# The retention stage of a nine-stage language tower: turns unrolled, normalising moved to groups of batches

## The chip, the cores and the metric

The kernel runs on one core of a Trainium2 chip. The metric is device time in microseconds (us), the median of several runs. The engines named below are TensorE (PE; its weight loads are PEld), VectorE (DVE), ScalarE (ACT), GpSimd (POOL) and SyncE (SP), whose queue issues the transfers (DMA) of this stage. SBUF is the on-chip memory, PSUM the banks that matmuls write.

## The reference, cut to what matters

The tower embeds 16 batches of 128 tokens with 192 features and adds eight blocks to them. The change is in the first of these, a retention block of 12 heads of 16 features:

```python
h = h + _L0_attn_ref(_layernorm(h, axis=-1), Wq, bq, Wk, bk, Wv, bv)

def proj(W, b):
    y = jnp.einsum('mse,fe->msf', x, W) + b
    return y.reshape(m, s, H, d).transpose(0, 2, 1, 3)
q, k, v = proj(Wq, bq), proj(Wk, bk), proj(Wv, bv)
decay = 1.0 / (1.0 + jnp.abs(i[:, None] - i[None, :]))
retention = jnp.einsum('mhsd,mhtd->mhst', q, k) * decay
out = jnp.einsum('mhst,mhtd->mhsd', retention, v) + k
mean = jnp.mean(out, axis=(2, 3), keepdims=True)
var = jnp.var(out, axis=(2, 3), keepdims=True)
out = (out - mean) / jnp.sqrt(var + EPS)
return out.reshape(m, s, e)
```

There is no softmax, so heads need no row maxima. Mean and variance are those of one head over all 128 tokens and 16 features. The last line reshapes (head, token, feature) into (token, feature) without turning it back, so that the rows of the result mix tokens of one head: this is what the exchange of heads is for.

## The kernel before, in words

Each stage of the program allocates its own tiles and semaphores, writes one program for each engine, and ends in a barrier of all engines. A normalising stage ahead of this one leaves the layer-normed rows transposed in `m.xt` (96 x 2 x 2048: features over partitions in two halves, tokens of all batches along the row). `retention_stage` then takes one batch a turn, 16 turns.

GpSimd copies the 128 columns of the batch from `m.xt` to `xs` (L848). TensorE's turn for batch b is `scores(b)`, `projections(b + 1)`, `outputs(b)`:

- `projections`: q and k, each three column groups by two halves of the features (L859, 12 records each, since a float32 matmul shows as two), and k with v beside it, token by feature, in `kv_ps` (L862, 4 records of 384 columns);
- `scores`: 12 matmuls with 16 rows, one for a head, at the partition offsets 0, 32, 64 and 96 (L872, 24 records);
- `outputs`: 12 matmuls of 128x128 weights and 16 columns (L882, 24 records), then the column sums of the normalisation through a matmul with `mean_w`, which holds 1/(128*16): the means after VectorE has summed (L886) and the variances after it has squared and summed (L889). Both wait on TensorE's queue, and what is behind them waits too.

VectorE's turn (`sequence`) multiplies the scores by the decay (L927, four operations), adds the three biases for the next batch (`biased`, L919 twice and L921), waits for outputs, adds k (L937), sums (L939), subtracts the mean (L941), squares (L942), sums (L943), adds epsilon (L945), takes the reciprocal of ScalarE's root (L909, L947), refines it (`newton_steps`, L156 to L160) and scales (L949). Then SP stores the batch's heads to DRAM in (head, token, feature) order (L837). After the last turn SP waits for all 16 stores and reads all of it back in the mixed order (L840), and VectorE adds it to the residual `m.h` (L959).

q, k and `ret` have one buffer each, `kv` two; `o` is one tile that each batch's store must leave before the next batch is written:

```python
v.wait_ge(o_ready, b + 1)
v.wait_ge(stored, 16 * b)
```

and outputs of b wait until b - 1 is normalised, since the means and variances lie in the same bank as the outputs:

```python
pe.wait_ge(ret_ready, b + 1)
pe.wait_ge(normed, b)
```

Of the kernel before, what the change touches and what calls it, by code (L numbers as in the profile page):

```python
# [11 lines left out]
ALU = mybir.AluOpType  # L12
# [784 lines left out]

def retention_stage(nc, m, a, scratch):
    with Stage(nc, "ret") as s:
# [8 lines left out]
        xs = s.sb("xs", [DC, 2, P])  # L808
# [4 lines left out]
        o = s.sb("o", [P, H0, HD0])  # L813
        sq = s.sb("sq", [P, H0, HD0])
        rs = s.sb("rs", [P, H0])
        rsq = s.sb("rsq", [P, H0])
        var, std = s.sb("var", [P, H0]), s.sb("std", [P, H0])
# [4 lines left out]
        w_in, xs_ready, proj_ready = s.sem("w_in"), s.sem("xs_ready"), s.sem("proj_ready")  # L822
        qkv_ready, sc_ready, ret_ready = s.sem("qkv_ready"), s.sem("sc_ready"), s.sem("ret_ready")
        o_ready, rs_ready, mean_ready = s.sem("o_ready"), s.sem("rs_ready"), s.sem("mean_ready")
        rsq_ready, var_ready, eps_added = s.sem("rsq_ready"), s.sem("var_ready"), s.sem("eps_added")
        std_ready, normed, stored = s.sem("std_ready"), s.sem("normed"), s.sem("stored")
        back_in, dve = s.sem("back_in"), s.sem("dve")
        block = s.block()

        @block.sync  # L830
        def _(sp):
            for dst, src in ((wq, "L0_wq"), (wk, "L0_wk"), (wkv, "L0_wkv"), (bq, "L0_bq"), (bk, "L0_bk"),
                             (bkv, "L0_bkv"), (decay, "decay"), (mean_w, "mean_w")):
                sp.dma_start(dst[:], a[src]).then_inc(w_in, 16)
            with sp.Fori(0, NB) as b:
                sp.wait_ge(normed, b + 1)
                sp.dma_start(scratch[bass.ds(b, 1)].rearrange("b h s d -> s (b h) d"), o[:]).then_inc(stored, 16)  # L837

            sp.wait_ge(stored, 16 * NB)
            sp.dma_start(back[:], scratch.rearrange("b h s d -> b (h s d)")  # L840
                         .rearrange("b (s e) -> s b e", e=D)).then_inc(back_in, 16)

        @block.gpsimd
        def _(pool):
            with pool.Fori(0, NB) as b:

                pool.wait_ge(proj_ready, b)
                nc.gpsimd.tensor_copy(xs[:], m.xt[:, :, bass.ds(b * P, P)]).then_inc(xs_ready, 1)  # L848

        @block.tensor  # L850
        def _(pe):
            pe.wait_ge(w_in, 16 * 8)
            def projections(b):
                pe.wait_ge(xs_ready, b + 1)
                pe.wait_ge(qkv_ready, b)
                for w, ps in ((wq, q_ps), (wk, k_ps)):
                    for g in range(HG):
                        for c in range(2):
                            nc.tensor.matmul(ps[:, g * P:(g + 1) * P], w[:, c, g * P:(g + 1) * P], xs[:, c, :],  # L859
                                             start=(c == 0), stop=(c == 1))  # L860
                for c in range(2):
                    last = nc.tensor.matmul(kv_ps[:, 0:2 * D], xs[:, c, :], wkv[:, c, :],  # L862
                                            start=(c == 0), stop=(c == 1))
                last.then_inc(proj_ready, 1)

            def scores(b):
                pe.wait_ge(qkv_ready, b + 1)
# [8 lines left out]
            def outputs(b, par):  # L876
                pe.wait_ge(ret_ready, b + 1)
                pe.wait_ge(normed, b)
                for g in range(HG):
                    for j in range(HJ):  # L880
                        hd = slice((g * HJ + j) * HD0, (g * HJ + j + 1) * HD0)
                        last = nc.tensor.matmul(o_ps[:, hd], ret[:, j, g * P:(g + 1) * P],  # L882
                                                kv[par][:, D + hd.start:D + hd.stop], start=True, stop=True)
                last.then_inc(o_ready, 1)
                pe.wait_ge(rs_ready, b + 1)
                nc.tensor.matmul(o_ps[:, 256:256 + H0], mean_w[:], rs[:], start=True, stop=True)\  # L886
                    .then_inc(mean_ready, 1)
                pe.wait_ge(rsq_ready, b + 1)
                nc.tensor.matmul(o_ps[:, 288:288 + H0], mean_w[:], rsq[:], start=True, stop=True)\  # L889
                    .then_inc(var_ready, 1)  # L890
# [8 lines left out]
            scores(NB - 2)  # L899
            projections(NB - 1)  # L900
            outputs(NB - 2, 0)
            scores(NB - 1)
            outputs(NB - 1, 1)

        @block.scalar
        def _(act):
            with act.Fori(0, NB) as b:
                act.wait_ge(eps_added, b + 1)
                nc.scalar.activation(std[:], var[:], ACT.Sqrt).then_inc(std_ready, 1)  # L909

        @block.vector
        def _(v):
            c = Chain(v, dve)
            v.wait_ge(w_in, 16 * 8)
            def biased(b, par):

                v.wait_ge(proj_ready, b + 1)
                for dst, ps, bias in ((q, q_ps, bq), (k, k_ps, bk)):
                    nc.vector.tensor_tensor(dst[:], ps[:, 0:HG * P].rearrange("p (g t) -> p g t", g=HG),  # L919
                                            along(bias[:], 2, [P, HG, P]), ALU.add)  # L920
                nc.vector.tensor_tensor(kv[par][:], kv_ps[:, 0:2 * D], bkv[:], ALU.add).then_inc(qkv_ready, 1)  # L921

            def sequence(b, par, more=True):
                c.round(b, 9)
# [7 lines left out]
                if more:  # L932
                    biased(b + 1, 1 - par)
                v.wait_ge(o_ready, b + 1)
                v.wait_ge(stored, 16 * b)
                heads = [P, H0, HD0]
                c.step(nc.vector.tensor_tensor(o[:], o_ps[:, 0:D].rearrange("p (h d) -> p h d", d=HD0),  # L937
                                               kv[par][:, 0:D].rearrange("p (h d) -> p h d", d=HD0), ALU.add))
                nc.vector.tensor_reduce(rs[:], o[:], AX.X, ALU.add).then_inc(rs_ready, 1)  # L939
                v.wait_ge(mean_ready, b + 1)  # L940
                c.step(nc.vector.tensor_tensor(o[:], o[:], along(o_ps[:, 256:256 + H0], 2, heads), ALU.subtract))  # L941
                c.step(nc.vector.tensor_tensor(sq[:], o[:], o[:], ALU.mult))  # L942
                nc.vector.tensor_reduce(rsq[:], sq[:], AX.X, ALU.add).then_inc(rsq_ready, 1)  # L943
                v.wait_ge(var_ready, b + 1)
                nc.vector.tensor_scalar(var[:], o_ps[:, 288:288 + H0], LN_EPS, None, ALU.add).then_inc(eps_added, 1)  # L945
                v.wait_ge(std_ready, b + 1)
# [2239 lines left out]
```

## Time and profile before

| | |
|---|---|
| Time, median of 3 runs | 3940.85 us (3937.39 to 3941.53) |
| Profiled execution | 3947.3 us, span 3945.4 us |
| Mean granted clock of TensorE | 0.806 |
| Busy, share of the span | PE 66%, PEld 41%, DVE 65%, ACT 38%, POOL 23% |
| Retention stage | from 67 us (first load issued) to 316 us (residual added) |

### The profile page before, as it was taken

The numbers are of one execution on the slowest core, as the hardware profiler recorded it, in microseconds if no ns is written. First come the engines' busy times: TensorE is split into PE (matmuls) and PEld (weight loads), VectorE is DVE, ScalarE is ACT, GpSimd is POOL, SyncE is SP. The second block draws the span as 40 slices with busy tenths as digits, with TensorE's granted clock in tenths as the row PEclk, the third lists the DMA queues.
The fourth block names the chain that finished last, engine by engine and source line by source line (L and its number), as shares of the span: only waits on it lengthen the run. The fifth ranks groups of instructions, "written<-read, shape, count | busy, mean of one in ns | idle before, by whom it ended". The sixth has DMA issues, their size and how long they took to land. (4 is left out here: it accounts for less than half of the span.)

```text
span 3945.4 us, 40861 instructions
## 1 busy us (share of the span) xinstructions
PE 2591.1 (66%) x13081; PEld 1614.0 (41%) x13128; DVE 2548.7 (65%) x5667; ACT 1513.9 (38%) x2746; POOL 895.5 (23%) x510
## 2 busy tenths in 40 slices
PE   2881999378888986599631112688989556665356
PEld 2771666233434333389411111323222445554345
DVE  4445232559999997211489997587787587787431
ACT  0000222166656652111114442677777244444211
POOL 2000000166776773367200000000000011011121
PEclk8775999689999997799855555899999777787568
DMA  1001100021111110511100000100000000000041
GB/s 34 8 7 39 67 0 0 28 86 43 43 43 43 43 43 0 148 40 39 46 0 0 0 0 1 50 1 1 1 1 1 28 1 1 1 1 1 25 133 48
DMA packets 59727, 108.45 MB, mean 27 GB/s; under 512 B 32253, under 2 KB 48091, under 8 KB 54331
## 3 DMA queue, kind: packets, MB, share of 16 engines
q1 hardware_dynamic: 53788, 94.44, 7.5%
q0 software_dynamic: 5760, 11.82, 1.0%
q8 instruction: 88, 1.44, 0.1%
q14 instruction: 91, 0.75, 0.1%
HBM read 92.17 MB, written 18.03 MB: 28 GB/s over the span
## 5 line engine op out<-in xcount | busy, mean ns | idle before, releaser
L1885 POOL TENSOR_TENSOR mam_st<-mam_du,mam_b_rows 128x1536 f32<-128x1536 f32 x128 | 439.4, 3439 | 172.1 <-PE mam_ysum L1954 171.6
L2115 DVE TENSOR_TENSOR_SCAN mam_st<-mam_da,mam_st 128x512 f32<-128x512 f32 x384 | 441.1, 1204 | 35.9 <-ACT mam_da L2055 18.2
L1650 DVE TENSOR_TENSOR cod_hp<-cod_hp,cod_gate 128x512 f32<-128x512 f32 x512 | 324.0, 681 | 122.5 <-ACT cod_hp L1517 120.5
L1954 PE MATMUL mam_ysum<-mam_st,held_ident 128*128 128x512 f32 x768 | 387.1, 644 | 2.2 <-DVE mam_st L2121 2.2
L1517 ACT ACTIVATE cod_hp<-cod_up,cod_b 128x512 f32<-128x512 f32 x512 | 318.8, 692 | 130.9 <-PE cod_up L1388 130.3
L2055 ACT ACTIVATE mam_da<-mam_delta,mam_decay 128x508 f32<-128x508 f32 x384 | 254.2, 683 | 184.7 <-DVE mam_st L2115 150.0
L2121 DVE TENSOR_TENSOR mam_st<-mam_st,mam_c_ps 128x1536 f32<-128x1536 f32 x128 | 224.4, 1753 | 17.2 <-PE mam_c_ps L1949 13.7
L470 DVE SCALAR_TENSOR_TENSOR held_h<-x_dn,held_gate,held_h 128x192 f32 x256 | 89.2, 410 | 225.2 <-PE x_dn L436 225.1
L1954 PEld LDWEIGHTS mam_ysum<-mam_st,held_ident 128*128 128x128 f32 x768 | 159.3, 207 | 169.3 <-issue 162.2
L425 PE MATMUL x_up<-x_xg,x_w 96*128 96x512 f32 x384 | 177.5, 600 | 55.4 <-ACTq L450 55.4
L311 POOL COPY held_xt<-n_cols 96x1024 f32 x32 | 34.3, 1074 | 776.3 <-ACT n_cols L292 776.3
L1388 PE MATMUL cod_up<-cod_zr,cod_w1r 96*128 96x512 bf16 x512 | 198.2, 387 | 15.6 <-ACT cod_hp L1517 9.7
L1393 PE MATMUL cod_gate<-cod_wt,cod_sel_g 128*128 128x512 bf16 x465 | 181.7, 391 | 39.3 <-DVE cod_hp L1650 38.7
L2390 DVE MATCH_REPLACE8 att_neg<-att_top,att_neg 128x128 f32<-128x128 f32 x768 | 201.1, 276 | 0.3 <-issue 0.3
L267 PE MATMUL n_turned<-held_ident,n_rows 128*96 128x128 f32 x256 | 51.4, 385 | 212.2 <-DVE n_rows L245 212.1
L2383 DVE MAX8 att_top<-att_neg 128x8 f32<-128x128 f32 x768 | 154.9, 279 | 22.6 <-ACT att_neg L2321 15.4
L2278 PE MATMUL att_wide<-held_ident,att_probs 128*128 128x128 f32 x192 | 45.1, 425 | 178.3 <-ACT att_probs L2333 178.3
L2227 POOL TENSOR_TENSOR att_probs<-att_se,att_neg 128x1536 f32<-128x1536 f32 x16 | 55.0, 3440 | 387.8 <-DVE att_neg L2390 387.8
L436 PEld LDWEIGHTS x_dn<-x_w,x_ht 128*128 128x128 f32 x768 | 128.2, 190 | 28.7 <-issue 28.7
L1409 PE MATMUL cod_comb<-cod_hp,cod_w 128*16 128x512 f32 x1024 | 137.2, 608 | 3.0 <-DVE cod_hp L1650 3.0
L458 ACT ACTIVATE x_ht<-x_up 128x512 f32<-128x512 f32 x96 | 57.3, 597 | 211.7 <-PE x_up L425 211.7
L436 PE MATMUL x_dn<-x_w,x_ht 128*128 128x192 f32 x768 | 134.7, 326 | 0.0
(519 smaller groups left out, 5443.4 us busy)
## 6 DMA issues: line engine op xcount, KB each, us to landing
mam_b_rows<-b_scratch SPq DMA_DIRECT2D x32, 1024.0 KB, 7.5
sw_w<-in_L_w SPq DMA_DIRECT2D x2, 4608.0 KB, 33.2
gr_w<-in_L_w SPq DMA_DIRECT2D x1, 5376.0 KB, 43.0
x_w<-in_L_w SPq DMA_DIRECT2D x2, 2304.0 KB
gr_w<-in_L_w SPq DMA_DIRECT2D x1, 4608.0 KB
slot_scratch<-in_slot_fresh SPq DMA_DIRECT2D x1, 3860.0 KB
gr_rows<-slot_scratch SPq DMA_DIRECT2D x40, 96.5 KB, 1.9
gr_w<-home_scratch SPq DMA_DIRECT2D x16, 192.0 KB, 4.4
```

Of the source, the lines that this page charges most:

```text
L425: last = nc.tensor.matmul(up[f % NUP][:], w1_sb[:, c, f, :], xg[:, c, :], start=(c == 0), stop=(c == 1))
L436: last = nc.tensor.matmul(dn[e % 2][:, t, 0:D], ht[e % 2][:, f, t * P:(t + 1) * P], w2_sb[:, f0 + f, :], start=(f == 0), stop=(f == tiles[ ...
L1388: nc.tensor.matmul(up[u % BANKS][:], w1r[:, sub, f * P:(f + 1) * P], zr[g % 2][:, sub, :], start=True, stop=True).then_inc(up_ready, 1)
L1393: nc.tensor.matmul(gate[u % BANKS][:], sel_g[:, code, :], wt[g % 2][:, 2 * sub + half, :], start=True, stop=True).then_inc(gate_ready, 1)
L1517: nc.scalar.activation(hp[step % HOLD][:, j, :], up[u % BANKS][:], ACT.Gelu_apprx_tanh, bias=b1[:, sub * HT + f:sub * HT + f + 1]).then_in ...
L1650: nc.vector.tensor_tensor(at, at, gate[u % BANKS][:], ALU.mult).then_inc(gated, 1)
L1885: nc.gpsimd.tensor_tensor(st[it % N_ST][:], du[r % 2][:], along(b_rows[:, p % RING, n % PIECE, :], 1, [P, MC, MT]), ALU.mult)\
L1954: last = nc.tensor.matmul(ysum[:, c, :], m.ident[:], st[it % N_ST][:, c, :], start=False, stop=(it % DS == DS - 1))
L2055: nc.scalar.activation(live(da[:, c, :], r % 2), live(delta[r % 2][:, c, :], r % 2), ACT.Exp, scale=decay[:, c, n:n + 1]).then_inc(exp_rea ...
L2115: nc.vector.tensor_tensor_scan(fs, fa, fs, 0.0, ALU.mult, ALU.add).then_inc(scanned, 1)
L2121: nc.vector.tensor_tensor(x[:], x[:], along(c_ps[:], 1, [P, MC, MT]), ALU.mult).then_inc(weighted, 1)
L2390: last = nc.vector.match_replace(rev, top[:, n, :], rev, -BIG)
```

## The change

All of it is in `retention_stage`.

- The loops over batches are written out. Batches form five groups (4, 4, 4, 2, 2), and `o` holds all 16 batches.
- TensorE reads `m.xt` in place; `xs` and GpSimd's program are gone.
- The biases of q and k are added by ScalarE while it copies out of PSUM (three operations of 128x128 each, a bias for each partition); kv's stays on VectorE. q, k and kv have semaphores of their own.
- A batch's outputs are only gathered in its turn. The sums of a group follow its last gather. Means on TensorE and `centre` on VectorE come in the turn after the group's last, variances, `roots` and `scaled` two turns after it, the addition to the residual four turns after it.
- SP stores the batches of a group when the group is scaled, waits for the stores, and reads the group back.
- The weights' loads are in another order, and q's matmuls wait only for `wq` and `bq`, k's for `wk` and `bk`.

```diff
+RET_GROUPS = (4, 4, 4, 2, 2)
...
+            for i in range(len(ends)):
+                sp.wait_ge(normed, i + 1)
+                for b in range(NB)[batches(i)]:
+                    sp.dma_start(scratch[b:b + 1].rearrange("b h s d -> s (b h) d"), o[:, b]).then_inc(stored, 16)
+                sp.wait_ge(stored, 16 * (ends[i] + 1))
+                sp.dma_start(back[:, batches(i), :], scratch[batches(i)].rearrange("b h s d -> b (h s d)")
+                             .rearrange("b (s e) -> s b e", e=D)).then_inc(back_in, 16)
-        @block.gpsimd
-        def _(pool):
-            with pool.Fori(0, NB) as b:
-
-                pool.wait_ge(proj_ready, b)
-                nc.gpsimd.tensor_copy(xs[:], m.xt[:, :, bass.ds(b * P, P)]).then_inc(xs_ready, 1)
...
-            def outputs(b, par):
+            def outputs(b):
                 pe.wait_ge(ret_ready, b + 1)
-                pe.wait_ge(normed, b)
+                pe.wait_ge(kv_kept, b + 1)
+                pe.wait_ge(o_added, b)
+                pe.wait_ge(mean_kept, sum(e <= b - 1 for e in ends))
+                pe.wait_ge(eps_added, sum(e <= b - 2 for e in ends))
...
+            pe.wait_ge(wq_in, 32)
             projections(0)
-            with pe.Fori(0, NB // 2 - 1) as i:
-                for par in range(2):
-                    b = 2 * i + par
-                    scores(b)
+            for b in range(NB):
+                scores(b)
+                if b - 1 in ends:
+                    means(ends.index(b - 1))
+                if b - 2 in ends:
+                    variances(ends.index(b - 2))
+                if b + 1 < NB:
                     projections(b + 1)
-                    outputs(b, par)
...
+            def keep_qk(b):
+                for dst, ps, bias, made, kept in ((q, q_ps, bq, q_made, q_kept), (k, k_ps, bk, k_made, k_kept)):
+                    act.wait_ge(made, b + 1)
+                    act.wait_ge(sc_ready, b)
+                    for g in range(HG):
+                        last = nc.scalar.activation(dst[:, g, :], ps[:, g * P:(g + 1) * P], ACT.Identity,
+                                                    bias=bias[:, g:g + 1])
+                    last.then_inc(kept, 1)
...
+            v.wait_ge(w_in, 64)
+            biased(0)
+            for b in range(NB):
+                decayed(b)
+                if b - 1 in ends:
+                    centre(ends.index(b - 1))
+                if b - 2 in ends:
+                    scaled(ends.index(b - 2))
+                if b - 4 in ends:
+                    add_back(ends.index(b - 4))
+                if b + 1 < NB:
+                    biased(b + 1)
+                gather(b)
+                if b in ends:
+                    sums(ends.index(b))
+            last = len(ends) - 1
+            centre(last)
+            scaled(last)
+            for i in range(len(ends)):
+                if ends[i] + 4 >= NB:
+                    add_back(i)
```

## Rows read from the trace of the kernel before

**Rows 1.** Windows: stretch, length, busy time (records) of each engine, PEclk, DMA share, GB/s.

```profile
108.00:135.00 27.00, 22.74 (x159) 20.80 (x158) 13.57 (x40) 0.42 (x2) 0.80 (x2) 0.75 0.06 7
```

**Rows 2.** Groups by shape, 64.5 to 318 us; after the second bar idle time before.

```profile
L927 DVE TENSOR_TENSOR ret_ret<-ret_sc,ret_decay 128x384 f32<-128x384 f32 x64 | 31.2, 550 | 1.7 <-PE ret_sc L872 1.5
...
L889 PE MATMUL ret_o_ps<-ret_rsq,ret_mean_w 128*128 128x12 f32 x32 | 9.6, 378 | 19.6 <-DVE ret_rsq L943 19.6
L919 DVE TENSOR_TENSOR ret_q<-ret_q_ps,ret_bq 128x384 f32<-128x384 f32 x16 | 8.9, 558 | 77.1 <-PE ret_kv_ps L862 77.1
...
L886 PE MATMUL ret_o_ps<-ret_rs,ret_mean_w 128*128 128x12 f32 x32 | 6.7, 283 | 14.7 <-DVE ret_rs L939 14.7
```

**Rows 3.** Timeline of one turn, TensorE's matmuls: start us, duration us.

```profile
109.87 1.66 PE L872 MATMUL ret_sc<-ret_q,ret_k 16*128 16x128 f32 x24
...
111.46 2.93 PE L859 MATMUL ret_q_ps<-ret_xs,ret_wq 96*128 96x128 f32 x12
...
114.18 2.40 PE L859 MATMUL ret_k_ps<-ret_xs,ret_wk 96*128 96x128 f32 x12
...
116.42 1.46 PE L862 MATMUL ret_kv_ps<-ret_wkv,ret_xs 96*128 96x384 f32 x4
...
117.71 2.75 PE L882 MATMUL ret_o_ps<-ret_kv,ret_ret 128*128 128x16 f32 x24
...
123.54 1.67 PE L872 MATMUL ret_sc<-ret_q,ret_k 16*128 16x128 f32 x24
```

**Rows 4.** Windows, short ones in which TensorE's granted clock moves.

```profile
81.50:82.00 0.50, 0.39 (x12) 0.39 (x16) 0.06 (x1) 0.00 (x0) 0.00 (x0) 0.92 0.00 0
...
88.80:92.20 3.40, 3.40 (x27) 2.97 (x25) 1.49 (x3) 0.00 (x0) 0.40 (x1) 0.99 0.00 0
92.40:95.60 3.20, 1.04 (x5) 0.83 (x5) 1.77 (x5) 0.00 (x0) 0.00 (x0) 0.50 0.00 0
...
116.00:116.50 0.50, 0.50 (x6) 0.50 (x6) 0.00 (x0) 0.00 (x0) 0.00 (x0) 0.95 0.00 0
...
123.00:123.50 0.50, 0.49 (x2) 0.49 (x2) 0.00 (x0) 0.00 (x0) 0.00 (x0) 0.50 0.00 0
```

**Rows 5.** Other stages: groups, a window and a timeline row of like operations.

```profile
L253 DVE TENSOR_TENSOR n2b_rows<-n2b_rows,n2b_shift 128x768 f32<-128x768 f32 x4 | 3.8, 958 | 0.1
...
L641 PE MATMUL gr_up<-gr_xs,gr_shared 97*128 97x128 f32 x960 | 115.1, 276 | 4.1 <-issue 4.1
...
1700.00:1800.00 100.00, 97.95 (x753) 95.00 (x752) 13.78 (x40) 19.44 (x40) 73.88 (x60) 1.00 0.14 41
...
2046.34 3.20 ACT L2712 ACTIVATE qh_x<-qh_sc,qh_down 128x128 f32<-128x128 f32 x12 [2.69 <-DVE qh_down L2783]
```

**Rows 6.** The stage's first microseconds: a window, then timeline rows.

```profile
69.00:70.00 1.00, 0.00 (x0) 0.00 (x0) 0.00 (x0) 0.00 (x0) 0.00 (x0) 0.50 1.03 323
...
73.20 2.93 PE L859 MATMUL ret_q_ps<-ret_xs,ret_wq 96*128 96x128 f32 x12 [9.30 <-DMA ret_mean_w<-in_mean_w]
...
78.49 1.47 PE L862 MATMUL ret_kv_ps<-ret_wkv,ret_xs 96*128 96x384 f32 x4
...
81.61 1.44 PE L872 MATMUL ret_sc<-ret_q,ret_k 16*128 16x128 f32 x24 [1.66 <-DVE ret_kv L921]
```

**Rows 7.** Timeline of the last batch and the exchange of heads.

```profile
291.45 5.31 PE L882 MATMUL ret_o_ps<-ret_kv,ret_ret 128*128 128x16 f32 x24 [2.46 <-DVE ret_ret L927]
296.79 0.36 DVE L937 TENSOR_TENSOR ret_o<-ret_o_ps,ret_kv 128x192 f32<-128x192 f32 x1 [5.40 <-PE ret_o_ps L882]
...
301.80 0.36 DVE L949 TENSOR_TENSOR ret_o<-ret_o,ret_rs 128x192 f32<-128x192 f32 x1
304.87 0.39 SPq L840 DMA_DIRECT2D ret_back<-heads_scratch  x1
312.63 3.36 DVE L959 TENSOR_TENSOR held_h<-held_h,ret_back 128x3072 f32<-128x3072 f32 x1 [10.47 <-DMA ret_back<-heads_scratch]
```

**Rows 8.** DMA: issues with size and median us to landing; one issue's duration.

```profile
gr_w<-home_scratch SPq DMA_DIRECT2D x16, 192.0 KB, 4.4
...
67.41 0.41 SPq L834 DMA_DIRECT2D ret_wk<-in_L_wk  x1
```

More of the change, by code:

```diff
@@ L795 @@
 HG, HJ = 3, 4
+RET_GROUPS = (4, 4, 4, 2, 2)
 def retention_stage(nc, m, a, scratch):
+    ends = [sum(RET_GROUPS[:i + 1]) - 1 for i in range(len(RET_GROUPS))]
     with Stage(nc, "ret") as s:
@@ L828, in retention_stage, with batches @@
         block = s.block()
+        def batches(i):
+            return slice(ends[i] + 1 - RET_GROUPS[i], ends[i] + 1)
         @block.sync
         def _(sp):
[L832 to L837, printed above, removed]
@@ L901, in _, with means, variances @@
-            outputs(NB - 2, 0)
-            scores(NB - 1)
-            outputs(NB - 1, 1)
+            def means(i):
+                n = RET_GROUPS[i] * H0
+                pe.wait_ge(rs_ready, i + 1)
+                nc.tensor.matmul(o_ps[:, 256:256 + n], mean_w[:], rs[:].rearrange("p b h -> p (b h)")[:, 0:n],
+                                 start=True, stop=True).then_inc(mean_ready, 1)
+            def variances(i):
+                n = RET_GROUPS[i] * H0
+                pe.wait_ge(rsq_ready, i + 1)
+                pe.wait_ge(o_added, min(ends[i] + 2, NB))
+                nc.tensor.matmul(o_ps[:, 320:320 + n], mean_w[:], rsq[:].rearrange("p b h -> p (b h)")[:, 0:n],
+                                 start=True, stop=True).then_inc(var_ready, 1)
@@ L905, in _ @@
+            pe.wait_ge(wq_in, 32)
+            projections(0)
+            for b in range(NB):
[5 more added lines that the diff above has]
+                if b + 1 < NB:
+                    projections(b + 1)
+                outputs(b)
+            means(len(ends) - 1)
+            variances(len(ends) - 1)
         @block.scalar
         def _(act):
-            with act.Fori(0, NB) as b:
-                act.wait_ge(eps_added, b + 1)
-                nc.scalar.activation(std[:], var[:], ACT.Sqrt).then_inc(std_ready, 1)
+            def keep_qk(b):
[6 more added lines that the diff above has]
+                    last.then_inc(kept, 1)
@@ L913, in _, with biased, decayed @@
             c = Chain(v, dve)
[L914 to L924, printed above, removed]
+            def biased(b):
+                v.wait_ge(kv_made, b + 1)
+                v.wait_ge(o_added, max(b - 1, 0))
+                nc.vector.tensor_tensor(kv[b % 2][:], kv_ps[:, 0:2 * D], bkv[:], ALU.add).then_inc(kv_kept, 1)
+            def decayed(b):
                 v.wait_ge(sc_ready, b + 1)
@@ L931, in sequence, with gather @@
                 last.then_inc(ret_ready, 1)
-                if more:
-                    biased(b + 1, 1 - par)
+            def gather(b):
                 v.wait_ge(o_ready, b + 1)
[L935 to L939, printed above, removed]
@@ L947, in sequence @@
-                c.step(nc.vector.reciprocal(rs[:], std[:]))
-                newton_steps(nc, c, rs[:], var[:], std[:])
-                nc.vector.tensor_tensor(o[:], o[:], along(rs[:], 2, heads), ALU.mult).then_inc(normed, 1)
-                c.end_round()
-            biased(0, 0)
-            with v.Fori(0, NB // 2 - 1) as i:
-                for par in range(2):
-                    sequence(2 * i + par, par)
-            sequence(NB - 2, 0)
-            sequence(NB - 1, 1, more=False)
-            v.wait_ge(back_in, 16)
@@ L959, in _, with sums @@
-            nc.vector.tensor_tensor(m.h[:], m.h[:], back[:], ALU.add)
+                nc.vector.tensor_tensor(o[:, b], o_ps[:, 0:D].rearrange("p (h d) -> p h d", d=HD0),
+                                        kv[b % 2][:, 0:D].rearrange("p (h d) -> p h d", d=HD0), ALU.add)\
+                    .then_inc(o_added, 1)
+            def sums(i):
+                n = RET_GROUPS[i]
+                v.wait_ge(o_added, ends[i] + 1)
+                nc.vector.tensor_reduce(rs[:, 0:n], o[:, batches(i)], AX.X, ALU.add).then_inc(rs_ready, 1)
@@ new lines, in centre @@
+            def centre(i):
+                n = RET_GROUPS[i]
+                heads = [P, n, H0, HD0]
+                x, part = o[:, batches(i)], sq[:, 0:n]
+                mean = o_ps[:, 256:256 + n * H0].rearrange("p (b h) -> p b h", h=H0)
+                v.wait_ge(mean_ready, i + 1)
+                nc.vector.tensor_copy(mid[:, 0:n], mean).then_inc(mean_kept, 1)
+                v.wait_ge(mean_kept, i + 1)
+                c.step(nc.vector.tensor_tensor(x, x, along(mid[:, 0:n], 3, heads), ALU.subtract))
+                c.step(nc.vector.tensor_tensor(part, x, x, ALU.mult))
+                nc.vector.tensor_reduce(rsq[:, 0:n], part, AX.X, ALU.add).then_inc(rsq_ready, 1)
```

95 lines of the change are left out of this document (55 added, 40 removed).

## The prediction

> **What bounds the kernel now.** I read the page first, and only to find the place: the retention stage runs from about 67 to 316 us of a span of 3945.4 us, so the change can touch 6% of the program, and everything below is read inside that stretch. Next I read the stretch by windows [rows 1]: in 27.00 us, two turns of the batch loop, TensorE is busy 22.74 us and VectorE 13.57 us, so TensorE sets the pace, at a mean granted clock of 0.75. Then the groups by shape [rows 2] show what its idle time is. The two small matmuls of the normalisation, means (L886) and variances (L889), are busy 6.7 + 9.6 us and TensorE sat idle 14.7 + 19.6 us ahead of them for VectorE: 50.6 us in 16 turns, 3.16 us of each. VectorE in its turn sat 77.1 us ahead of L919 for the projections; it is no bound. Then one turn in order of time [rows 3]: scores 109.87, q projection 111.46, k 114.18, kv 116.42, outputs 117.71 to 120.46, the two small matmuls, and the next scores at 123.54: a turn of 13.67 us. Last the half-microsecond windows [rows 4], for the clock: TensorE runs scores, q and k at 0.50 of full speed (1.2 GHz), the grant goes to 1.00 (2.4 GHz) at 116, deep in the dense projections, and it is back at 0.50 before the next scores.
>
> **The change, part by part.** The chain that sets the end goes from the weights' landing through TensorE's 16 turns to the exchange of heads. Three stretches are to be summed: front, turns, tail.
>
> *Front.* Before, q waits until all eight loads have landed, at 73.20, while the queues move 323 GB/s [rows 6]. Now wq and bq come first and have a semaphore of their own. 288 KB at some 300 GB/s are 1 us behind the first traffic at 68, with bq behind it 69.5 to 70.5; k waits for wk and kv for the rest, each due while the part before it runs. So TensorE starts at about 70.2 instead of 73.2. Also the first scores started at 81.61, 1.65 us after kv had ended at 79.96, for VectorE's three bias additions; q and k now go to ScalarE as each is made, behind which the kv matmuls still run, and scores do not wait for kv's bias. 3.0 + 1.65 would be 4.6; I take 4.1, between 1.6 (the loads share the engines so that nothing lands early) and 4.7.
>
> *A turn of TensorE at either level of clock.* At the low level, from [rows 3, 7]: scores 1.6, q and k 2.7 + 2.5 (k's 2.24 ended at the high level), outputs 5.3 (the last batch, 291.45), kv twice its 1.29 at the high level, 2.6; together 14.7 us. At the high level: outputs 2.75 and kv 1.29 [rows 3], scores 0.78 (12 of 24 records in 0.39 [rows 4]), and q with k 24 records of 0.120 each, which is what 960 records of almost the same shape cost in another stage at a granted 1.00, 115.1 us [rows 5], so 2.88. Together 7.7 us. None of it changes in number: the same matmuls, read from the held transposed rows in place of the copy. The copy lay under scores and TensorE never waited for it; without it nothing is gained.
>
> *What leaves the turn.* Outputs of batch b no longer wait for b-1 to be normalised, and the small matmuls come once for a group, behind scores of the next turn. What is left of the 3.16 us: four times, means wait for the sums (after outputs, gather 0.36 [rows 7] and a sum over 768 elements, about 0.96 by the row of that size [rows 5], while scores run 0.8 to 1.6), then their two records and those of the variances, 0.4 to 0.6 each [rows 2]: 1.6 us for each of the four groups that end before the last turn, 6.4 us in all (1.2 to 1.9 each).
>
> *What VectorE now does.* Per batch: decay, four of 0.49 [rows 2], 1.95; kv bias 0.55, as L919; gather 0.36 [rows 7]. Per group of four: five operations over 768 elements and a share of the addition to the residual, six at 0.96 [rows 5], and some nine small ones of 0.17 to 0.25 with 0.04 between, 2.0, so 7.8, or 1.95 a batch. Sum 4.8, with the gaps 5.1 us a turn: below 7.7. The fullest turn (centring) has 1.95 + 0.17 + 2.9 + 0.55 + 0.36 = 5.9 and also fits. Behind centring stand the bias of kv and the gather; outputs of b+1 wait for both, a projection's length later. Outputs of b wait for the decay of b, 2.0 us behind scores, and the projections between last 4.2 or more. So the removed stall is not made again, except in turn 15, which has no projections: there scores, then a wait of 2.4 for decay and for the epsilon of the group before, then outputs, much as now [rows 7].
>
> *ScalarE* gets six 128x128 additions of a bias a turn. Twelve like it took 3.20 us elsewhere, 0.27 each [rows 5]: 1.6 us a turn on an engine that has only one root a turn now. The root of a group is queued ahead of the q and k of that turn and waits for VectorE until some 2.5 us behind scores; the last k is then kept 4.3 us behind scores, at the high level 3.4 us before the next scores ask. Cost nothing; if that cover were gone, 1 us in each of four turns.
>
> *SP's queue* carries the same 16 stores plus five reads back in place of one; each group's wait for its stores holds only SP, where the next store comes two turns later. Nothing but the last group's is on the path. The loops' removal is worth at most the 0.2 us of weight loads' issue a turn, which lies under matmuls; taken at nothing. That unrolled code feeds TensorE is seen in a stage written out flat: busy 97.95 of 100 us at 1.00 [rows 5].
>
> *The clock* is the unknown. If TensorE goes on at the mean of before, 0.75 [rows 1], a turn is 7.7/0.75 = 10.3 us, which agrees with 13.65 - 3.16 = 10.5. Its idle time is gone, though, and the dense projections return sooner, which speaks for more; against all of it speaks that between 88.8 and 92.2 TensorE was busy for the whole 3.40 us, the end of kv and then outputs with 16 columns each, and the next window reads 0.50 [rows 4]. Outputs and scores together are 3.5 us of such work in every turn. I take the middle of 7.7 and 10.3, 9.0 us, that is, one drop in most turns but a short one. The Trainium skill (TensorE: Matmul & The Clock Gate, Part 1) says that the low clock is the idle state and that sustained activity releases it. By that rule alone a TensorE that never idles is at the high level throughout; the row of 88.8 to 92.2 disagrees, and it is a rival below.
>
> *Turns, summed.* 15 x 9.0 = 135.0; four groups 6.4; last turn 1.6 + 2.4 + 4.0 = 8.0: 149.4 us from first scores to last outputs. Before: 81.61 to 296.76, 215.1 [rows 6, 7]. Gain 65.7.
>
> *Tail.* Before, 296.76 to 315.99 [rows 7], 19.2: 5.4 of normalising, store 2.7 with its handing over, read of all 16 batches 7.8, addition 3.36. Now two batches are normalised: five operations of 384 elements in place of 192 at +0.2 (0.56 for 384 in L919, 0.36 for 192 in L937 [rows 2, 7]) and one copy of 0.2, 6.6; two stores, 0.45 for the second's issue [rows 8] + 2.7, 3.1; a read of 192 KB, 3.2 (between the store's 2.7 for 96 KB [rows 7] and 4.4 for another read of 192 KB [rows 8]); addition 0.56. 13.5, gain 5.7 (4.4 to 6.5). Twelve batches' exchange and addition lie under turns.
>
> *Sum.* 65.7 + 4.1 + 5.7 = 75.5. The profiled execution took 3947.3 us (span 3945.4), so 3871.8 by its measure; the median of the runs is 3940.85, 6.4 lower, which the profiled one exceeds in stages the change leaves alone, so 3865.3: I say **3865 us**.
>
> **The rivals.** (1) *High clock throughout.* 15 x 7.7 = 115.5, groups 5.2, last turn 0.8 + 2.4 + 2.75 = 5.95: 126.7, gain 88.4 + 9.8 = 98.2, **3843 us**. For it: no idle time on TensorE, the flat stage at 1.00. Against: the drop after 88.8 to 92.2. (2) *The clock stays at three quarters.* 15 x 10.3 + 14.4 = 168.9, gain 46.2 + 9.8 = 56.0, **3885 us**. For it: the level falls in outputs and comes back only late in dense projections [rows 4], and both are in each turn still. (3) *A new wait on VectorE.* If centring, scaling and the kv bias queued ahead of the decay made outputs wait as in the last turn, 2.4 us a turn: 15 x 12.7 + 14.4 = 204.9, gain 10.2 + 9.8 = 20, **3921 us**. VectorE's 5.1 of 7.7 us speak against it. (4) *Slower.* The clock stays low: the one idle stretch that now never comes does not matter, but outputs and scores, nearer to each other, keep the grant at 0.50 in every turn. 15 x 14.7 + 6.8 + 9.3 = 236.6, 21.5 more, less 9.8: **3953 us**. It decides from a turn of 14.0 us on, so only when hardly any of the time is at the high level. Against it: at 116, as in each turn, dense projections did lift it [rows 4]. (5) *The change doesn't unhook the turns* (turn still 13.65, since some other wait ties outputs to the normalising): gain 9.8, **3931 us**.
>
> **How the numbers follow.** Forecast 0.42, (1) 0.21, (2) 0.25, (3) 0.05, (4) 0.03, (5) 0.03; 0.01 for the rest. The range from 3840 to 3888 takes the first three with the bounds of front (1.6 to 4.7), groups and tail; that is 0.88 less their own edges. A measurement of this kernel tells about 0.2%, 8 us, from no change: all of the first three and (3) and (5) are faster by more; between (5) and (4) lies what is within it. Faster 0.94, same 0.02, slower 0.04.
>
> **What would show it.** No idle time of TensorE ahead of the small matmuls but in four turns (some 3 us in all, 34.3 before); turns of 7.7 to 10.5 us, falling together with the granted clock of their window; VectorE's idle time, now ahead of the gather, for outputs; the first q at about 70; the last read landing 3 us after its issue, 6 us after the last scaling. I am wrong if the granted clock of the stage stays at 0.75 or goes to 1.00, if ScalarE loads a table between roots and additions, or if outputs wait for decay outside of the last turn.

## The result and the profile after

The changed kernel takes 3873.2 us (median of 4 runs, 3866.7 to 3882.2), the kernel before 3941.2 (4 runs); the ratio is 0.9828 with a 95% interval of 0.9805 to 0.9851. 3865 was predicted, in a range of 3840 to 3888. The profiled execution has a span of 3869.1 us, 76.3 shorter than before; 3871.8 was predicted for its own time, which is 3871.3.

The retention stage, from the issue of its first load to the last addition to the residual, went from 249.0 us (67.00 to 315.99) to 176.6 (67.61 to 244.18), 72.4 us less. It splits into the prediction's three stretches:

| stretch | before | after | gain | predicted |
|---|---|---|---|---|
| front: first load issued to first scores | 14.6 | 10.6 | 4.0 | 4.1 |
| turns: first scores to end of last outputs | 215.2 | 152.5 | 62.7 | 65.7 |
| tail: end of last outputs to residual added | 19.2 | 13.5 | 5.7 | 5.7 |

The stretch of the turns, as windows (stretch, length, busy time of PE, PEld, DVE, ACT and POOL with records, granted clock, DMA share, GB/s), of the kernel after:

```profile
78.20:225.40 147.20, 144.74 (x1181) 133.40 (x1181) 68.93 (x142) 27.07 (x94) 0.00 (x0) 0.80 0.11 17
```

It answers to [rows 1]. TensorE is busy 144.7 of 147.2 us, where it was busy 22.74 of 27.00; its records number the same but for the small matmuls. The mean grant (the granted clock, as a share of full speed) went only from 0.74 or 0.75 to 0.80. VectorE is busy 68.9 us, 4.6 a turn. What is left of the small matmuls, by shape, with the idle time ahead of them behind the second bar:

```profile
L965 DVE TENSOR_TENSOR ret_o<-ret_o_ps,ret_kv 128x192 f32<-128x192 f32 x16 | 5.7, 357 | 34.4 <-PE ret_o_ps L888 34.4
...
L895 PE MATMUL ret_o_ps<-ret_rs,ret_mean_w 128*128 128x48 f32 x6 | 2.0, 426 | 0.6 <-DVE ret_rs L972 0.6
L902 PE MATMUL ret_o_ps<-ret_rsq,ret_mean_w 128*128 128x48 f32 x6 | 1.5, 338 | 0.0
```

The 34.3 us of idle time ahead of L886 and L889 [rows 2] are 0.6 us in the turns of the groups of four, and none for the first group of two (the last group's fall in the tail); VectorE now waits for outputs, 34.4 us. Two turns in order of time, one at the high level throughout and one in which it is lost (start us, duration us), answer to [rows 3]:

```profile
105.91 0.95 PE L875 MATMUL ret_sc<-ret_q,ret_k 16*128 16x128 f32 x24
...
106.79 1.60 PE L855 MATMUL ret_q_ps<-held_xt,ret_wq 96*128 96x128 f32 x12
...
108.24 1.50 PE L855 MATMUL ret_k_ps<-held_xt,ret_wk 96*128 96x128 f32 x12
...
109.58 1.46 PE L864 MATMUL ret_kv_ps<-ret_wkv,held_xt 96*128 96x384 f32 x4
...
110.87 2.75 PE L888 MATMUL ret_o_ps<-ret_kv,ret_ret 128*128 128x16 f32 x24
...
113.55 0.95 PE L875 MATMUL ret_sc<-ret_q,ret_k 16*128 16x128 f32 x24
...
115.05 0.63 PE L895 MATMUL ret_o_ps<-ret_rs,ret_mean_w 128*128 128x48 f32 x2 [0.56 <-DVE ret_rs L972]
115.48 2.89 PE L855 MATMUL ret_q_ps<-held_xt,ret_wq 96*128 96x128 f32 x12
...
118.17 2.77 PE L855 MATMUL ret_k_ps<-held_xt,ret_wk 96*128 96x128 f32 x12
...
120.73 2.06 PE L864 MATMUL ret_kv_ps<-ret_wkv,held_xt 96*128 96x384 f32 x4
...
125.31 1.67 PE L875 MATMUL ret_sc<-ret_q,ret_k 16*128 16x128 f32 x24
```

Windows, first of an earlier turn, then of these two:

```profile
85.85:95.49 9.64, 9.64 (x77) 8.95 (x76) 2.86 (x6) 1.76 (x6) 0.00 (x0) 0.78 0.01 2
105.90:113.50 7.60, 7.60 (x77) 6.94 (x76) 2.86 (x6) 1.76 (x6) 0.00 (x0) 1.00 0.01 2
113.50:125.30 11.80, 11.24 (x80) 10.16 (x79) 6.70 (x11) 1.76 (x6) 0.00 (x0) 0.71 0.00 1
```

A turn at the high level is 7.64 us (7.7 predicted). The one with a drop is 11.8; of the 4.1 us between them 1.0 is the small matmul and the wait for it (scores end at 114.50, q starts at 115.48), the rest the clock. The turn of the first row, 85.85 to 95.49, has no small matmul, the same 77 records as the high one and TensorE busy throughout: there the clock alone makes 9.64 of 7.64. By the starts of scores the 15 turns are 7.6 us (four of them) and 9.5 to 11.8 (eleven). The front and the tail, against [rows 6, 7]:

```profile
70.82 2.93 PE L855 MATMUL ret_q_ps<-held_xt,ret_wq 96*128 96x128 f32 x12 [6.30 <-DMA ret_bq<-in_L_bq]
...
78.22 0.95 PE L875 MATMUL ret_sc<-ret_q,ret_k 16*128 16x128 f32 x24
...
225.42 5.28 PE L888 MATMUL ret_o_ps<-ret_kv,ret_ret 128*128 128x16 f32 x24 [1.92 <-DVE ret_var L992]
...
237.53 1.12 SPq L842 DMA_DIRECT2D heads_scratch<-ret_o  x2
241.22 0.36 SPq L844 DMA_DIRECT2D ret_back<-heads_scratch  x1
243.62 0.56 DVE L1000 TENSOR_TENSOR held_h<-held_h,ret_back 128x384 f32<-128x384 f32 x1 [5.65 <-DMA ret_back<-heads_scratch]
```

q starts 3.2 us behind the first load's issue (6.2 before). Normalising the last two batches takes 6.8 us, the two stores 3.7, reading back 2.4, the addition 0.56.

### The profile page after: what moved, and what is told of

The parts are those of the page before. It is cut to its first block and busy times, and to the rows that moved or that the text cites. A ratio compares the mean times of both kernels' runs of the same rounds, so it can differ in the third digit from the quotient of the medians.

```text
span 3869.1 us, 40336 instructions
## 1 busy us (share of the span) xinstructions
PE 2558.3 (66%) x13037; PEld 1582.9 (41%) x13084; DVE 2514.2 (65%) x5512; ACT 1539.9 (40%) x2831; POOL 888.7 (23%) x494
## 5 line engine op out<-in xcount | busy, mean ns | idle before, releaser
L2445 DVE MAX8 att_top<-att_neg 128x8 f32<-128x128 f32 x768 | 154.8, 278 | 21.9 <-ACT att_neg L2383 15.1
```

## The experiments

All ran the whole program beside runs of the kernel before. "Turns" is, in the traces, from first scores to the start of the last outputs: 209.8 us before (81.61 to 291.45), 147.2 after. Ratios are to the kernel before.

### 1. The deferral undone

```diff
-RET_GROUPS = (4, 4, 4, 2, 2)
+RET_GROUPS = (1,) * 16
...
                 outputs(b)
+                means(b)
+                variances(b)
...
                 gather(b)
+                sums(b)
+                centre(b)
+                scaled(b)
```

> The changed kernel with the deferral undone and all else kept (written out, rows in place, biases on ScalarE, heads exchanged by group, here groups of one): means and variances follow each batch's outputs on TensorE and VectorE normalises in the turn. Nothing left out. Theory A (what gained in the turns is TensorE no longer idling for VectorE): TensorE idles 30 to 36 us ahead of the small matmuls again, granted clock near 0.75, turns of 13.0 to 13.8 us, from first scores to last outputs 205 to 216 us where the change has 152.5, the whole 3925 to 3937. Rival C (the other parts carry half of the gain or more): turns of 11.5 us or less, the whole 3905 or less.

3934.4 us, ratio 0.9976 (0.9966 to 0.9987). Windows over the turns, of the kernel before first and then of this one, and this one's small matmuls with the idle time ahead of them:

```profile
81.61:291.45 209.84, 175.06 (x1225) 159.90 (x1225) 103.57 (x304) 3.19 (x15) 5.56 (x14) 0.74 0.06 7
...
77.10:285.70 208.60, 172.03 (x1226) 156.83 (x1225) 95.23 (x302) 29.63 (x105) 0.00 (x0) 0.73 0.09 15
...
L902 PE MATMUL ret_o_ps<-ret_rsq,ret_mean_w 128*128 128x12 f32 x32 | 9.6, 378 | 23.0 <-DVE ret_rsq L978 23.0
L895 PE MATMUL ret_o_ps<-ret_rs,ret_mean_w 128*128 128x12 f32 x32 | 6.9, 290 | 13.4 <-DVE ret_rs L966 13.4
```

208.6 us to the start of the last outputs, 213.9 to their end: within 1.2 us of before, with the grant at 0.73 and TensorE idle 36.4 us for VectorE again. Unrolling, reading in place and ScalarE's biases together are worth at most these 1.2 us in the turns. What remains, 9 us of the medians (3943.6 to 3934.4), is front and tail; in the trace the front is 4.6 us shorter than before and the tail 8.8. The deferral is the gain in the turns, all but that 1.2 us.

### 2. Biases on VectorE, the copy restored, groups of two

```diff
+                for dst, ps, bias, made, kept in ((q, q_ps, bq, q_made, q_kept), (k, k_ps, bk, k_made, k_kept)):
+                    v.wait_ge(made, b + 1)
+                    v.wait_ge(sc_ready, b)
+                    nc.vector.tensor_tensor(dst[:], ps[:, 0:HG * P].rearrange("p (g t) -> p g t", g=HG),
+                                            along(bias[:], 2, [P, HG, P]), ALU.add).then_inc(kept, 1)
                 v.wait_ge(kv_made, b + 1)
```

> The changed kernel with the biases of q and k back on VectorE, ahead of kv's; ScalarE has the roots alone. Nothing left out. Theory A (VectorE has 5.1 us of work in a turn of 9.25 and does not set the pace): VectorE busy about 16 us less idle, turns the same within 0.1 us, first scores 1.5 us later, the stage 0 to 4 us longer than 176.6. Rival D (VectorE would become the bound, so this part earned something): outputs wait for decay or bias in turns that centre or scale, the stage 10 us longer or more.

3875.1 us, ratio 0.9826 (0.9809 to 0.9843).

```diff
+            for b in range(NB):
+                pool.wait_ge(kv_made, b)
+                nc.gpsimd.tensor_copy(xs[:], m.xt[:, :, b * P:(b + 1) * P]).then_inc(xs_ready, 1)
...
-                                                    m.xt[:, c, at], start=(c == 0), stop=(c == 1))
+                                                    xs[:, c, :], start=(c == 0), stop=(c == 1))
```

> The changed kernel with GpSimd's copy of the batch's transposed rows back, read by the projections in place of the held rows. Nothing left out. Theory A (the copy always lay under scores and outputs): TensorE waits for it nowhere but at the first batch, where the loads hide it; turns as in the change, 146 to 153 us from first scores to last outputs, the whole 3868 to 3886. Rival (reading in place earned something, by a wait or a port): 5 us or more on the turns beyond 153.

3884.3 us, ratio 0.9853 (0.9829 to 0.9877).

```diff
-RET_GROUPS = (4, 4, 4, 2, 2)
+RET_GROUPS = (2,) * 8
```

> The changed kernel with eight groups of two batches in place of 4, 4, 4, 2, 2. Nothing left out. Theory A (the lag takes the normalisation off TensorE's path; the size of a group only sets how often the small matmuls are issued): three more pairs of them at 1.0 to 1.6 us, 3 to 5 us in the turns, drowned by the clock's scatter of 6 us; the whole 3868 to 3890. Rival (grouping by four is what makes VectorE fast enough): outputs wait for VectorE, 10 us or more.

3881.4 us, ratio 0.9838 (0.9814 to 0.9862). Windows over the turns of the three, in fences of their own, biases on VectorE first, then the copy, then groups of two:

```profile
76.80:229.80 153.00, 149.47 (x1182) 137.09 (x1181) 84.10 (x172) 0.89 (x4) 0.00 (x0) 0.77 0.11 17
```

```profile
76.70:229.70 153.00, 149.46 (x1182) 136.98 (x1181) 68.70 (x142) 27.22 (x94) 6.47 (x15) 0.77 0.11 17
```

```profile
77.60:224.50 146.90, 144.54 (x1193) 133.48 (x1192) 75.11 (x184) 27.40 (x97) 0.00 (x0) 0.81 0.10 17
```

VectorE has 15.2 us more with the biases (84.1 against 68.9) and the turns do not feel it more than they feel the copy. First scores come 9.8 us behind the first load's issue with the biases on VectorE, no later than with the change (10.6), so that part of my expectation missed. Some 1.0 us of this is the clock, which rose earlier there: k and kv of the first batch took 2.45 and 1.46 us, and 2.77 and 2.19 in the change's trace. What mattered at the front seems to be that q and k are biased each as it is made, under the matmuls that follow, and not which engine does it; no run biases them late to show it. Groups of two show no price above the scatter that experiment 3 looks at.

### 3. The ends undone, and the change once more

```diff
+            pe.wait_ge(wk_in, 32)
+            pe.wait_ge(w_in, 64)
             projections(0)
...
+            sp.wait_ge(stored, 16 * NB)
+            sp.dma_start(back[:], scratch.rearrange("b h s d -> b (h s d)")
+                         .rearrange("b (s e) -> s b e", e=D)).then_inc(back_in, 16)
...
+            v.wait_ge(back_in, 16)
+            nc.vector.tensor_tensor(m.h[:], m.h[:], back[:], ALU.add)
```

> The changed kernel with its two ends undone: all eight loads are waited for in the old order before the first matmul, and the heads are read back and added in one piece behind the last batch. Turns untouched, nothing left out. Theory A: first q 2.0 to 2.7 us later, from last outputs to the end of the stage 19.5 to 21 us in place of 13.5, turns the same within the clock's own scatter (2 us in all), the stage 8 to 10 us longer. Rival E (the exchange by group disturbs the turns by its stores and reads, or costs the tail nothing because the last read's latency is fixed): the turns 3 us or more shorter without it, or the tail less than 3 us longer.

3890.0 us, ratio 0.9865 (0.9848 to 0.9881). First q 6.5 us behind the first load's issue, 3.3 later than with the change; from the start of the last outputs to the end of the stage 26.5 us (232.86 to 259.40) against 18.8: 7.8 more. The turns, untouched, were 153.0 us where the change's trace has 147.2, so:

> The changed kernel once more, unedited, for the scatter of its turns: two kernels whose turns were untouched had 152.9 us from first scores to the start of the last outputs, the change's own trace 147.2. If that is the clock's scatter from one execution to the next, this trace lies between 145 and 155 us and the median near 3873; if the change's trace was typical and the two others were slowed by their edits, it is 147 again.

3883.6 us, ratio 0.9855 (0.9838 to 0.9872): the change's own medians lie 10 us apart and its gains 8 (68.0 and 59.8 us), so no difference of that size between medians here tells anything. Its turns took 146.5 us; windows of the change once more, then of the ends undone:

```profile
77.20:223.70 146.50, 143.00 (x1181) 131.16 (x1180) 68.69 (x142) 27.18 (x94) 0.00 (x0) 0.81 0.11 17
```

```profile
79.90:232.90 153.00, 149.46 (x1182) 137.02 (x1181) 66.93 (x140) 27.19 (x94) 0.00 (x0) 0.77 0.08 9
```

Six profiles of turns with the same work on TensorE fall into two sets, 146.5 to 147.2 at 0.80 or 0.81 and 153.0 at 0.77. In the first are both profiles of the unedited kernel and groups of two; in the second are the biases on VectorE, the copy and the ends undone. Three edits with nothing in common landed on the same 153.0, which speaks for the clock's scatter rather than for the edits. The single turns, by the starts of scores, say more. In the three kernels of the second set and in the change once more the last eleven turns are the same to 0.03 us (10.1, 7.9, 9.3, 7.6, 11.8, 11.6, 10.3, 7.6, 11.7, 11.0, 9.9), so none of the three edits costs anything there. The whole difference lies in turns 2 to 4: 9.3, 7.6 and 9.3 us in the change once more, 10.9, 11.1 and 10.5 in the three. The change's first trace and groups of two have other orders of turns, whose sums happen to be near. Why those three turns differ stays open: with both unedited profiles in the other set, one profile of each can't settle it. With it set aside, the ends are worth 11 us in the traces, 3.3 and 7.8, somewhat more than I expected; the medians have 16.8 or 6.5, by which median of the change is taken.

### 4. The order of the dense work

kv's projection goes from ahead of the outputs to behind them, and on VectorE the gather ahead of kv's bias with it (not shown below); the operations are the same.

```diff
                 if b + 1 < NB:
                     projections(b + 1)
                 outputs(b)
+                if b + 1 < NB:
+                    kv_projection(b + 1)
```

> The changed kernel, with kv's projection of the next batch moved from before this batch's outputs to behind them, and the gather put ahead of kv's bias on VectorE. Same operations, nothing left out. Theory A (the clock falls because outputs and scores, some 3.5 us of narrow matmuls, stand together; 1.3 us of dense work between them breaks that stretch up): mean granted clock from first scores to last outputs 0.90 or more where it was 0.79, turns of 7.7 to 8.3 us in place of 9.25, the stage 14 to 22 us shorter than 176.6, the whole near 3855. Rival B (only how much dense work a turn holds counts, or only idle time, not the order): granted clock 0.77 to 0.82, the stage within 4 us of 176.6, the whole near 3873.

3925.7 us, ratio 0.9962 (0.9950 to 0.9974): some 50 us slower than the biases on VectorE (3875.1), which ran on the same chip and have the change's order on TensorE. Neither theory had that. Windows over its turns, then over a single one:

```profile
77.10:271.40 194.30, 192.60 (x1182) 166.49 (x1181) 69.07 (x142) 27.33 (x94) 0.00 (x0) 0.59 0.08 13
```

```profile
118.50:133.60 15.10, 15.10 (x79) 13.21 (x78) 5.85 (x10) 1.77 (x6) 0.00 (x0) 0.50 0.00 1
```

TensorE is busy 192.6 of 194.3 us, and the grant is 0.59. The second row is a turn wholly at the low level, 15.1 us: the 14.7 of the prediction and a small matmul. Its timeline:

```profile
118.51 1.67 PE L878 MATMUL ret_sc<-ret_q,ret_k 16*128 16x128 f32 x24
...
120.57 2.89 PE L855 MATMUL ret_q_ps<-held_xt,ret_wq 96*128 96x128 f32 x12
123.25 2.77 PE L855 MATMUL ret_k_ps<-held_xt,ret_wk 96*128 96x128 f32 x12
125.81 5.14 PE L891 MATMUL ret_o_ps<-ret_kv,ret_ret 128*128 128x16 f32 x24
130.79 2.91 PE L867 MATMUL ret_kv_ps<-ret_wkv,held_xt 96*128 96x384 f32 x4
```

Q and k (dense work: wide matmuls one behind the other) are 5.3 us in one piece, kv 2.9 apart from them, and in this turn the level stays low from scores to scores. It is not so in every turn:

```profile
108.55 2.93 PE L855 MATMUL ret_q_ps<-held_xt,ret_wq 96*128 96x128 f32 x12
111.27 2.52 PE L855 MATMUL ret_k_ps<-held_xt,ret_wk 96*128 96x128 f32 x12
113.62 2.75 PE L891 MATMUL ret_o_ps<-ret_kv,ret_ret 128*128 128x16 f32 x24
116.22 2.35 PE L867 MATMUL ret_kv_ps<-ret_wkv,held_xt 96*128 96x384 f32 x4
```

Here the level came back at the end of k, and was lost again within kv. By the starts of scores the first two turns are 7.7 us, six are 11.5 to 12.0 with such a return, and seven 14.4 to 15.1 with none. In the change the three projections stand together; after the level fell at 115, q and k at 115.5 to 120.7 and kv behind them brought it back (kv 2.06 us, outputs 2.75), and no turn is longer than 11.8. So I had looked at one side only: at what lets the level fall. The order also bears on whether it comes back. A new theory from this: the narrow matmuls make it fall, and dense work in one piece lifts it again, the surer the longer the piece.

### 5. Wide outputs: more work in less time

Each outputs matmul streams up to 128 columns instead of the 16 that it needs. Later heads write over the surplus, so the result stands.

```diff
-                        hd = slice((g * HJ + j) * HD0, (g * HJ + j + 1) * HD0)
+                        at = (g * HJ + j) * HD0
+                        hd = slice(at, min(at + P, D))
```

> The changed kernel with more work on TensorE and nothing else: each of the 12 outputs matmuls of a batch streams up to 128 columns (from its head's first column to the end of v) in place of 16. The later heads write over the surplus, so the same numbers stand at the end; nothing is left out. Their weight loads, some 0.115 us a record at the high level, set their pace, so the columns should cost 0.1 to 0.3 us a turn. Theory F (the grant follows how many columns TensorE streams, and it falls because outputs stream hardly any): mean granted clock from first scores to last outputs 0.93 or more in place of 0.79, turns 7.8 to 8.4 us, the stage 15 to 23 us shorter than 176.6, the whole 3850 to 3860. Rival G (being busy is what counts, narrow or wide): grant 0.77 to 0.82, the stage the same or 2 to 5 us longer.

3861.2 us, ratio 0.9802 (0.9782 to 0.9821), on the same chip as the change's 3883.6: 22 us faster for more columns, as are its turns in the traces (124.6 us against 146.5 and 147.2).

```profile
78.00:202.60 124.60, 120.84 (x1182) 110.21 (x1181) 68.42 (x142) 26.91 (x94) 0.00 (x0) 0.97 0.13 20
```

```profile
147.20 2.97 PEld L889 LDWEIGHTS ret_o_ps<-ret_kv,ret_ret 128*128 128x128 f32 x24
147.53 2.75 PE L889 MATMUL ret_o_ps<-ret_kv,ret_ret 128*128 128x128 f32 x24
```

The grant is 0.97, the turns 124.6 us, and the 24 records still last 2.75 us, as with 16 columns; the columns lie under the weight loads, which fill the same stretch. Two turns took 10.1 us: both have the means of a group, with their wait ahead of them, so wide outputs didn't keep the level in those. Then wide outputs and kv behind them:

> Both edits: kv's projection behind the outputs, which alone took the turns from 147 to 194 us, and the outputs matmuls up to 128 columns wide. Nothing left out. Theory F: with wide outputs the whole of a turn but scores is dense, so the order no longer matters, turns 7.8 to 8.6 us, the whole 3850 to 3865, some 65 us faster than the order alone with narrow outputs. Rival (the order cost something other than the clock, a wait or the weights' order): still above 3910.

3853.8 us, ratio 0.9778 (0.9760 to 0.9796).

```profile
77.60:198.30 120.70, 118.78 (x1182) 104.62 (x1181) 69.09 (x142) 26.88 (x94) 0.00 (x0) 1.00 0.14 21
```

The order that alone cost 50 us is now the fastest of all, 72 us under the same order with narrow outputs and 30 under the change on the same chip. The grant is 1.00 throughout, a turn 7.8 us (117.5 us from first scores to last scores, in 15), small matmuls included. That is about the 7.7 us and the groups' 5.2 of the prediction's first rival. Scores stayed narrow in both kernels; what they do to the level by themselves was not tried.

### 6. Thin work in small pieces, and wide outputs alone

Outputs one turn later, in three pieces behind q, k and kv; narrow.

```diff
-        ret = s.sb("ret", [P, HJ, HG * P])
+        ret = [s.sb(f"ret{i}", [P, HJ, HG * P]) for i in range(2)]
...
                     last.then_inc(made, 1)
+                    between(0 if w is wq else 1)
...
                 last.then_inc(kv_made, 1)
+                between(2)
...
+                    projections(t + 1, lambda g: outputs(t - 1, g))
```

> The changed kernel with outputs of a batch one turn later, in three pieces of four heads behind q, k and kv of the next projections, narrow as in the change; decayed scores in two buffers, means and variances a turn later too. Same operations, nothing left out. Theory F with a floor: once the high level is reached (the first projections reach it) no stretch without dense work is longer than a third of outputs and scores, 1.7 us, in place of 3.5, so the grant stays high: turns 7.7 to 8.2 us, the whole 3848 to 3862. Rival H (the mix is still too thin, and once the level has fallen no dense stretch is long enough at the low level to lift it, as with kv behind outputs): turns of 11 us or more, the whole above 3900.

3899.6 us, ratio 0.9872 (0.9845 to 0.9900), with its ten runs from 3867.5 to 3937.6, far wider apart than any other kernel's. The profile shows both expectations in one execution:

```profile
78.30:146.00 67.70, 67.14 (x680) 60.70 (x683) 32.04 (x67) 16.13 (x55) 0.00 (x0) 1.00 0.08 13
146.00:236.00 90.00, 89.83 (x484) 80.68 (x478) 31.49 (x65) 11.07 (x38) 0.00 (x0) 0.50 0.12 18
```

For 67.7 us the grant is 1.00; then it falls, once, and for the next 90.0 us of the same turns it is 0.50 and does not come back. Around the fall:

```profile
145.00:145.50 0.50, 0.50 (x6) 0.48 (x5) 0.00 (x0) 0.00 (x0) 0.00 (x0) 1.00 0.00 0
145.50:146.00 0.50, 0.50 (x16) 0.49 (x19) 0.36 (x1) 0.00 (x0) 0.00 (x0) 0.93 0.00 0
146.00:146.50 0.50, 0.50 (x19) 0.50 (x12) 0.49 (x1) 0.00 (x0) 0.00 (x0) 0.50 0.00 0
```

TensorE is busy throughout: the level falls in scores, behind a piece of outputs, a mix that eight turns before it had run at 1.00. This is experiment 4 seen from its other side: the mix that ran at the high level for 67.7 us did not restore it in 90.

Last, wide outputs as the only edit of the kernel before:

> The kernel before, with one edit: its outputs matmuls stream up to 128 columns in place of 16. Nothing left out, all of the change's parts absent. Theory F (columns hold the grant): its granted clock from first scores to last outputs rises from 0.74, but the 2.2 us in which TensorE waits for the normalisation and the scores behind it still stand together in every turn, so the level should still fall in many: turns of 11.0 (always high: 7.7 + 3.2) to 13.0 us, the whole 3900 to 3932. Rival (the idle time alone makes it fall, once a turn, whatever the outputs stream): turns stay 13.65 us, the whole 3938 to 3945.

3940.3 us, ratio 0.9989 (0.9979 to 0.9999).

```profile
81.30:290.90 209.60, 174.74 (x1224) 159.68 (x1224) 103.57 (x304) 3.18 (x15) 5.57 (x14) 0.74 0.06 7
```

The rival was right: turns of 13.7 us (from first scores to last, in 15) and a grant of 0.74 as before. With the normalisation still in the turn, the level falls in each turn, with wide outputs as with narrow ones.

## Why the prediction was right, step by step

- **What bounds it** held: TensorE, idle for the normalisation. Putting that back alone (experiment 1) gave the turns back, 208.6 us of 209.8.
- **The parts costed at nothing** show no price that can be told from the scatter: the copy, ScalarE against VectorE for the biases, the unrolling, the groups' size (experiments 1 and 2). No table load shows among ScalarE's records of the stage.
- **VectorE's load**, 5.1 us a turn with its gaps, was 4.6 busy; outputs waited for it in the last turn only.
- **Small matmuls**: 1.6 us a group were predicted, 6.4 in all; by the rows of after 5.1 (idle 0.6, busy 2.0 and 1.5 for the groups of four, busy 0.6 and 0.4 for the first group of two).
- **The front**: 4.0 us against 4.1, but put together otherwise. q started 3.0 us earlier relative to the first load, as said; the rest I had put down to ScalarE; experiment 2 has it with VectorE as well, so the engine is not the reason.
- **The tail**: 13.5 us against 13.5, from terms that missed both ways: normalising 6.8 (6.6), stores 3.7 (3.1), reading back 2.4 (3.2).
- **The clock** was the unknown, taken as the middle, 9.0 us a turn between 7.7 and 10.3. It was 9.26 ((144.0 - 5.1) / 15): 3.9 us more in 15 turns, which with 1.3 less for the small matmuls and 0.5 more in the last turn (8.5) is the 3 us by which the turns fell short. "One drop in most turns but a short one" is what the trace shows, in eleven of fifteen. That it came to 9.26 and not to 8 or 10 was luck: no row gave the middle, and the same work took 9.2 in the change once more and 9.6 in the three kernels of 153.0. The median of the change once more, 3883.6, is 19 us above the forecast and only just inside the range. The reason given, that outputs and scores pull the level down while TensorE is busy, held for outputs (experiment 5); the scores' part was not tried. What the prediction lacked is the way back: experiments 4 and 6 show that with TensorE as busy as it can be, the same operations in another order take 194.3 us of turns, and that narrow work in small pieces can stay at 0.50 for 90 us.
- **The rivals.** High clock throughout (3843) was reached by no kernel with narrow outputs; with wide ones it was, and the turns then took 120.7 us to the start of the last outputs, near that rival's 124. Three quarters of the clock (3885) was close by in experiments 2 and 3 at 0.77. The slower rival's mechanism, outputs and scores keeping the level low in a busy TensorE, is real: kv behind outputs, at 0.59, is most of the way to it, and the change with that one step in the other order would have gained 18 us (3943.6 to 3925.7) and not 68.
- By the rule of the Trainium skill that sustained activity releases the low clock (TensorE: Matmul & The Clock Gate, Part 1) the turns would have run high in every version whose TensorE is never idle. Experiment 4 disagrees, with TensorE busy 192.6 of 194.3 us at a mean grant of 0.59, and so does the change's turn from 85.85; the measurement decides.

In the profiles the whole moved by 76.3 us and the stage by 72.4; the medians moved by 68.0. The next stage does not explain the 3.9 us between the first two, since it took 3.6 us more after the change (window 245.0 to 335.9, 90.9 us against 87.3, TensorE busy 17.4 us for 96 records against 14.2). So some 8 us were gained in stages that the change leaves alone. That is within the runs' spread of 15 us and was not followed; what the stage gained is known by its own window, and from the medians to some 8 us only.

## What to carry to other kernels

Take what makes TensorE wait for another engine out of its queue by one turn, before moving any work between engines: here the deferral was all but 1.2 us of the gain in the turns. When TensorE is then always busy, its clock can still halve. What helped here was to put narrow matmuls, whose weight loads set the pace, at full width where the surplus is harmless; what cost 50 us was to split the dense stretch while the narrow one was left. Look at the granted clock of each order tried, not at the busy share, which read 98 to 99% at 0.59 and at 1.00 alike.

## What the hardware showed that I had not expected

- 24 outputs records last 2.75 us at the high level with 16 columns and with up to 128. With the wider ones the grant was 0.97 in the change's order and 1.00 with kv behind them, where the narrow ones had 0.80 and 0.59.
- Two levels for the same work: in one execution turns of the same operations ran 67.7 us at 1.00 and the next 90.0 us at 0.50, with no idle time where the level fell.
- Four kernels, one of them the change itself, ran the same eleven turns, 7.6 to 11.8 us long, to 0.03 us alike, and differed by 6.4 us in the three turns ahead of them. What picks those is open.
